# Layer 1 attention heads: TensorE's projections and scores in another order

## The chip, the cores and the metric

The kernel runs on one core of one Trainium2 chip. The metric is the device time of one execution in microseconds (us), given as the median of several runs. The five engines of the core work through their own instruction lists in order and meet at semaphores: PE is TensorE (matmuls, and PEld its weight loads), DVE is VectorE, ACT is ScalarE, POOL is GpSimd and SP issues the DMAs.

## The reference, cut to what matters

Four transformer layers follow one another, each an attention block and a feed-forward block on a normalised x. The change touches only the attention of layer 1: 16 heads of 128 features, on one sequence of 1024 tokens with 256 features, with rotary embedding and a window of 128 tokens.

```python
q = split_heads(hidden_states @ wq)
k = split_heads(hidden_states @ wk)
v = split_heads(hidden_states @ wv)
q = _apply_rotary(q, cos, sin)
k = _apply_rotary(k, cos, sin)
attn = jnp.einsum('bhqd,bhkd->bhqk', q, k) * scale
attn = jnp.where(valid, attn, neg)          # valid: the 128 keys up to the query
attn = jax.nn.softmax(attn, axis=-1)
out = jnp.einsum('bhqk,bhkd->bhqd', attn, v)
return out @ wo
```

## The kernel before, in words

The order of everything is written out by hand, one list for each engine. The 16 heads of layer 1 are a loop over pairs of heads. `c` is 0 for the even head of a pair and 1 for the odd one. While head h is finished, the queries and keys of head h+1 are made, so one pass of `head` holds steps of two heads. The last head has no next one.

On TensorE these are the steps of one pass:

- `project_qk(h + 1, j)`, j = 0 to 3: keys of tokens 0 to 511 (j = 0), queries of the same tokens (1), keys and queries of tokens 512 to 1023 (2, 3). Each is six matmuls of 512 columns on fp32r operands (a value is split in a high and a low part, three products for each half of the 256 features; lines 486 to 488). It writes bank j % 2, so only banks 0 and 1 of PSUM are used: j = 2 must find bank 0 read out, j = 3 bank 1. That is the wait on `rope_half`, which VectorE raises.
- `scores(h, gs)`, four groups g of 256 queries, in fp32, into bank 2 + g % 2 (line 649). Groups 0 and 1 of head h are made in the pass before, groups 2 and 3 in its own.
- `turn_probs(h, g)`: transposes of the exponentials (line 663), into bank 4 or 5.
- `weigh_values(h, ..., g)`: probabilities times values in fp32 (lines 678, 679), into bank 6 or 7.
- `project_out(h, p)`, four parts of six fp32r matmuls of 256 columns, and in the odd heads `project_v` of the next pair, four parts of twelve (lines 486 to 488 again).

VectorE's list for one pass is: `row_max(h, 2)`, `rotate(h + 1, 0)`, `row_max(h, 3)`, `rotate(h + 1, 1)`, in the heads 0 to 9 a step of the expert selection of layer 1 (`choose`), `rotate(h + 1, 2)`, `rotate(h + 1, 3)`, the reciprocal, `rest_of_oT` twice, `row_max(h + 1, 0)` and `(h + 1, 1)`, in the heads 0 to 9 a second `choose` step, and four `add_head`, which add the head's output to x. `row_max` (line 1406) takes a group of scores out of its bank. `rotate` (lines 1396 and 1397) reads a projection out of bank j % 2 and raises `rope_half` when it is done; it also waits for ScalarE's `keep_raw` (line 1030), a copy of the same bank. GpSimd adds the two halves of the rotation (lines 1733, 1738) and raises `qk_ready`, for which the scores wait.

ScalarE's list is: exponentials of group 0 and 1 (line 1049), `keep_raw(h + 1, 0)`, exponentials of group 2, `keep_raw(h + 1, 1)`, `keep_pT` 0 and 1, exponentials of group 3, `keep_raw` 2, `keep_pT` 2, `keep_raw` 3, `keep_oT` 0, `keep_pT` 3, `keep_oT` 1.

Of the kernel before, what the change touches and what calls it, by code (L numbers as in the profile page):

```python
# [81 lines left out]
def build(nc, dram, out):  # L82

    ctx = ExitStack()
    with ctx:
# [48 lines left out]
        def parts(pair):  # L134

            return [t.bitcast(F32R) for t in pair]
# [25 lines left out]
        def first(n):  # L162

            return isinstance(n, int) and n == 0
# [281 lines left out]
        def _(pe):  # L446
# [32 lines left out]
            def tok(t):  # L479
                return slice(t * P, (t + 1) * P)  # L480

            def split_product(dst, terms, open_end=False):


                for n, ((lhi, llo), (rhi, rlo)) in enumerate(terms):
                    pe.matmul(dst, lhi, rhi, start=(n == 0), stop=False)  # L486
                    pe.matmul(dst, lhi, rlo, start=False, stop=False)  # L487
                    last = pe.matmul(dst, llo, rhi, start=False, stop=(n == len(terms) - 1 and not open_end))  # L488
                return last

            def cut(pair, *at):
                return [t[at] for t in pair]
# [122 lines left out]
            def project_qk(h, j, pair=None):  # L615

                mm, b = 1 - j % 2, j // 2
                if j == 0:
                    pe.wait_ge(wqk_split, h + 1)
                if j < 2 and pair is not None:  # L620
                    pe.wait_ge(v1_ready, pair * 4 + (3 + j))
                elif j >= 2 or not first(h):
                    pe.wait_ge(rope_half, h * 4 + (j - 1))
                split_product(ps[j % 2], [(cut(parts(wqk2), ALL, tok(mm * KD + k)), cut(parts(xT1), ALL, k, slice(b * BW, (b + 1) * BW)))
                                          for k in range(KD)]).then_inc(qk_full, 1)

            def project_v(pair, p):

                if p == 0:
                    pe.wait_ge(wv_split, pair + 1)  # L630
                if p < 2:
                    pe.wait_ge(rope_half, pair * 8 + (3 + p))
                else:
                    pe.wait_ge(v1_ready, pair * 4 + (p - 1))
                for tt in range(2):
                    last = split_product(ps[p % 2][:, tt * D:(tt + 1) * D], [(cut(parts(xT1), ALL, k, tok(2 * p + tt)), cut(parts(wv2), ALL, k))
                                                                             for k in range(KD)])
                last.then_inc(v_full, 1)

            def scores(h, gs):  # L640

                for g in gs:
                    pe.wait_ge(qk_ready, h * 4 + (2 if g < 2 else 4))
                    if g >= 2:
                        pe.wait_ge(smax_ready, h * 4 + (g - 1))
                    for tt in range(2):
                        t = 2 * g + tt
                        lo = P if t == 0 else 0
                        last = pe.matmul(ps[2 + g % 2][:, tt * 2 * P + lo:(tt + 1) * 2 * P], qT1[:, tok(t)],  # L649
                                         kT1[:, t * P - P + lo:t * P + P], start=True, stop=True)  # L650
                    last.then_inc(bank_full[2 + g % 2], 1)

            def turn_probs(h, g):
                pe.wait_ge(exp_done, h * 4 + (g + 1))
                if g < 2:
                    pe.wait_ge(x_added, h * 4 + (HEAD0["added"] - 1 + g))
                else:
                    pe.wait_ge(pT_ready, h * 4 + (g - 1))
                for tt in range(2):
                    for s in range(2):  # L660
                        t = 2 * g + tt
                        if t or s:
                            last = pe.transpose(ps[4 + g % 2][:, tok(2 * tt + s)], S1[:, t, tok(s)], ident)  # L663
                last.then_inc(bank_full[4 + g % 2], 1)

            def weigh_values(h, pair, c, g):

                mine = slice(c * DH, (c + 1) * DH)
                pe.wait_ge(pT_ready, h * 4 + (g + 1))
                if g % 2 == 0:  # L670
                    pe.wait_ge(*HEAD0["left"][6 + g // 2])
                    pe.wait_ge(x_added, h * 4 + (HEAD0["added"] - 3 + g // 2))
                if g == 0:
                    pe.wait_ge(v1_ready, pair * 4 + 4)
                for tt in range(2):
                    t = 2 * g + tt
                    if t:
                        pe.matmul(ps[6 + g // 2][:, tok(t % TPB)], v1[:, t - 1, mine], pT1[:, t, 0, :], start=True, stop=False)  # L678
                    last = pe.matmul(ps[6 + g // 2][:, tok(t % TPB)], v1[:, t, mine], pT1[:, t, 1, :], start=(t == 0), stop=True)  # L679
                if g % 2:  # L680
                    last.then_inc(bank_full[6 + g // 2], 1)

            def project_out(h, p):

                if p == 0:
                    pe.wait_ge(wo_split, h + 1)
                if p < 2:
                    pe.wait_ge(oT1_ready, h * 2 + (p + 1))
                if p == 2:
                    pe.wait_ge(oT1_ready, h * 2 + 2)  # L690
                bank = OUT1[p]
                for tt in range(2):
                    last = split_product(ps[bank][:, tt * D:(tt + 1) * D], [(cut(parts(oT1), ALL, tok(2 * p + tt)), parts(wo2p))])
                last.then_inc(bank_full[bank], 1)

            def head(pair, c, more=True, more_v=True):

                h, next_pair = pair * 2 + c, None if c else pair
                if more:
                    project_qk(h + 1, 0, next_pair)  # L700
                scores(h, [2])
                if more:
                    project_qk(h + 1, 1, next_pair)
                turn_probs(h, 0)
                turn_probs(h, 1)
                scores(h, [3])
                if more:
                    project_qk(h + 1, 2)
                weigh_values(h, pair, c, 0)
                turn_probs(h, 2)  # L710
                if more:
                    project_qk(h + 1, 3)
                weigh_values(h, pair, c, 1)
                turn_probs(h, 3)
                weigh_values(h, pair, c, 2)
                weigh_values(h, pair, c, 3)
                if c and more_v:
                    project_v(pair + 1, 0)
                if more:
                    scores(h + 1, [0, 1])  # L720
                for p in range(NT // 2):
                    project_out(h, p)
                    if c and more_v and p < NT // 2 - 1:
                        project_v(pair + 1, p + 1)
# [26 lines left out]
            with pe.Fori(0, H1 // 2 - 1) as i:  # L751
                for c in range(2):
                    head(i, c)
            head(H1 // 2 - 1, 0)
            head(H1 // 2 - 1, 1, False, False)


# [1176 lines left out]
```

## Time and profile before

| | before |
|---|---|
| median of 3 runs | 828.32 us (827.7, 828.32, 833.49) |
| span of the profiled execution | 825.5 us |
| mean granted TensorE clock over the span | 0.968 |
| PE busy | 751.2 us, 91% of the span |
| DVE, ACT, POOL busy | 554.4, 371.9, 339.0 us |

The profiled execution is told by its span, from its first to its last instruction; the time of that same execution around the span is not given apart. The median of the runs is 2.8 us above this span. All times below are in microseconds from the start of the span. The passes of heads 0 to 14, those with a next head, run from 257.78 to 560.8. TensorE counts as busy nearly without a break there, but its matmuls are pipelined and the ends of its records are modelled, so that a record's duration can cover a wait; the starts of consecutive records tell more.

### The profile page before, as it was taken

The numbers are of one execution on the slowest core, as the hardware profiler recorded it, in microseconds if no ns is written. First come the engines' busy times: TensorE is split into PE (matmuls) and PEld (weight loads), VectorE is DVE, ScalarE is ACT, GpSimd is POOL, SyncE is SP. The second block draws the span as 40 slices with busy tenths as digits, with TensorE's granted clock in tenths as the row PEclk, the third lists the DMA queues.
The fourth block names the chain that finished last, engine by engine and source line by source line (L and its number), as shares of the span: only waits on it lengthen the run. The fifth ranks groups of instructions, "written<-read, shape, count | busy, mean of one in ns | idle before, by whom it ended". The sixth has DMA issues, their size and how long they took to land.

```text
span 825.5 us, 12512 instructions
## 1 busy us (share of the span) xinstructions
PE 751.2 (91%) x4180; PEld 590.4 (72%) x4180; DVE 554.4 (67%) x1101; ACT 371.9 (45%) x783; POOL 339.0 (41%) x250
## 2 busy tenths in 40 slices
PE   6999999999979999999999999998999799766467
PEld 2456676667838898989898999997889446455356
DVE  4454554632269979797979675755566844499995
ACT  2554111101146565656565656555455441475541
POOL 0000364420046757575757584843111110337661
PEclk9999999999999999999999999999999999977798
DMA  8300000000040100010100010101110000100001
GB/s 315 154 0 1 1 1 1 1 1 0 1 147 2 27 25 27 24 28 23 28 23 27 24 51 6 33 7 37 41 38 0 0 1 0 33 0 1 0 1 51
DMA packets 11167, 24.33 MB, mean 29 GB/s; under 512 B 1217, under 2 KB 5442, under 8 KB 10626
## 3 DMA queue, kind: packets, MB, share of 16 engines
q1 hardware_dynamic: 10832, 23.02, 8.3%
q10 hardware_dynamic: 306, 0.92, 0.5%
q8 instruction: 18, 0.29, 0.1%
q14 instruction: 11, 0.09, 0.0%
HBM read 22.89 MB, written 1.05 MB: 29 GB/s over the span
## 4 chain that ended last, share of the span: by engine, by line
PE 68%; DVE 21%; issue 7%; ACT 2%; DMA 1%; POOL 1%; DVEq 1%; SPq 0%; ACTq 0%; POOLq 0%
PE bank L467 11%; PE bank L486 8%; PE bank L488 8%; PE bank L487 8%; PE bank L476 7%; PE bank L649 4%; PE bank L556 3%; PE bank L542 3%; PE bank L679 2%; PE bank L504 2%; PE bank L678 2%; DVE x L1422 2%; PE bank L663 2%; PE bank L525 2%; DVE arena L1396 2%
## 5 line engine op out<-in xcount | busy, mean ns | idle before, releaser
L486 PE MATMUL bank<-zone 128*128 128x256 f32 (+1 forms) x520 | 180.2, 346 | 9.2 <-DVE arena L1397 3.9
L488 PE MATMUL bank<-zone 128*128 128x256 f32 (+1 forms) x520 | 169.5, 326 | 0.0
L487 PE MATMUL bank<-zone 128*128 128x256 f32 (+1 forms) x520 | 169.3, 326 | 0.0
L486 PEld LDWEIGHTS bank<-zone 128*128 128x128 f32 x520 | 99.2, 191 | 26.7 <-DVE arena L1397 9.4
L1733 POOL TENSOR_TENSOR arena<-arena 128x512 f32<-128x512 f32 x64 | 82.2, 1284 | 84.4 <-ACT arena L1030 75.5
L488 PEld LDWEIGHTS bank<-zone 128*128 128x128 f32 x520 | 99.1, 191 | 8.7
L487 PEld LDWEIGHTS bank<-zone 128*128 128x128 f32 x520 | 99.4, 191 | 6.6
L1738 POOL TENSOR_TENSOR arena<-arena 128x512 f32<-128x512 f32 x64 | 82.4, 1288 | 33.1 <-DVE arena L1397 23.0
L1727 POOL TENSOR_TENSOR zone<-arena,zone 128x512 fp32r<-128x512 f32 (+1 forms) x56 | 58.6, 1059 | 58.9 <-ACT zone L1092 46.2
L467 PE MATMUL bank<-xT,arena 128*128 128x512 f32 x160 | 77.1, 611 | 0.0
L1049 ACT ACTIVATE arena<-arena 128x256 f32<-128x256 f32 (+1 forms) x128 | 62.1, 487 | 32.9 <-DVE arena L1406 32.8
L1710 POOL TENSOR_TENSOR lnw<-lnw,minus_half 128x4 f32<-128x4 f32 x8 | 8.1, 1015 | 134.8 <-DVE lnw L1234 134.8
L1422 DVE SCALAR_TENSOR_TENSOR x<-bank,arena,x 128x256 f32<-128x256 f32 x128 | 53.0, 471 | 15.0 <-PE bank L488 14.7
L1406 DVE CUSTOM_DVE_ANT_0 arena<-bank,const 128x256 f32<-128x256 f32 (+1 forms) x128 | 46.2, 403 | 24.4 <-PE bank L649 24.2
L869 PE MATMUL bank<-zone 128*128 128x512 f32 x128 | 39.2, 463 | 25.4 <-DVE arena L1609 21.4
L649 PE MATMUL bank<-arena 128*128 128x256 f32 (+1 forms) x256 | 59.8, 366 | 0.0
L1396 DVE TENSOR_TENSOR arena<-bank,arena 64x512 f32<-64x512 f32 x64 | 44.3, 693 | 16.3 <-ACT arena L1030 14.8
L869 PEld LDWEIGHTS bank<-zone 128*128 128x128 f32 x128 | 27.9, 226 | 35.3 <-DVE arena L1609 23.8
L1719 POOL TENSOR_TENSOR arena<-arena 128x1024 bf16<-128x1024 bf16 x6 | 12.8, 2128 | 95.3 <-DVE arena L1343 95.3
L979 ACT ACTIVATE arena<-bank 128x512 f32<-128x512 f32 x16 | 9.6, 597 | 90.8 <-PE bank L467 90.8
L679 PE MATMUL bank<-arena 128*128 128x128 f32 x256 | 49.5, 275 | 0.7 <-ACT arena L1017 0.7
L1030 ACT ACTIVATE arena<-bank 128x512 f32<-128x512 f32 x64 | 37.5, 586 | 24.9 <-PE bank L488 24.9
(268 smaller groups left out, 1530.4 us busy)
## 6 DMA issues: line engine op xcount, KB each, us to landing
arena<-in_qk SPq DMA_DIRECT2D x16, 256.0 KB, 2.7
arena<-in_tern SPq DMA_DIRECT2D x1, 3072.0 KB, 20.3
arena<-in_wv SPq DMA_DIRECT2D x8, 256.0 KB, 2.6
arena<-in_wo SPq DMA_DIRECT2D x16, 128.0 KB, 2.0
arena<-in_w SPq DMA_DIRECT2D x8, 256.0 KB, 2.7
lB<-in_lB SPq DMA_DIRECT2D x1, 1288.5 KB, 22.9
arena<-in_lA SPq DMA_DIRECT2D x1, 1282.5 KB, 13.6
x<-in_x SPq DMA_DIRECT2D x1, 1024.0 KB, 11.0
```

Of the source, the lines that this page charges most:

```text
L467: last = pe.matmul(g.ps, weight(k), act[:, k, b * BW:(b + 1) * BW], start=(k == 0), stop=(k == KD - 1))
L486: pe.matmul(dst, lhi, rhi, start=(n == 0), stop=False)
L487: pe.matmul(dst, lhi, rlo, start=False, stop=False)
L488: last = pe.matmul(dst, llo, rhi, start=False, stop=(n == len(terms) - 1 and not open_end))
L649: last = pe.matmul(ps[2 + g % 2][:, tt * 2 * P + lo:(tt + 1) * 2 * P], qT1[:, tok(t)], kT1[:, t * P - P + lo:t * P + P], start=True, stop= ...
L679: last = pe.matmul(ps[6 + g // 2][:, tok(t % TPB)], v1[:, t, mine], pT1[:, t, 1, :], start=(t == 0), stop=True)
L869: last = pe.matmul(g.ps, weight, part[:, k, b * BW:(b + 1) * BW], start=(k == 0 and m == 0), stop=(k == KD - 1 and m == 1))
L1049: last = act.activation(S1[:, t, lo:], S1[:, t, lo:], ACT.Exp, scale=-1.0, bias=nmax[:, t:t + 1], accum_out=rsum[:, t:t + 1])
L1396: dve.tensor_tensor(qsin[0:64, j, :], ps[j % 2][64:128, :], sinT[64:128, at], ALU.mult)
L1422: last = dve.scalar_tensor_tensor(out=x[:, t, :], in0=ps[bank][:, tt * D:(tt + 1) * D], scalar=rinv[:, t:t + 1], in1=x[:, t, :], op0=ALU.m ...
L1733: pool.tensor_tensor(qraw[:, j, :], qraw[:, j, :], cosT[:, at], ALU.mult).then_inc(cos_done, 1)
L1738: pool.tensor_tensor((kT1, qT1)[j % 2][:, at], qraw[:, j, :], qsin[:, j, :], ALU.add).then_inc(qk_ready, 1)
```

## The change

Only TensorE's list is touched; the other engines' lists, the semaphores, the buffers and every matmul stay as they are. Three things move in a pass: `project_qk` 1 comes right behind `project_qk` 0, ahead of the score group 2; `project_qk` 3 comes right behind `project_qk` 2, ahead of `weigh_values` 0 and `turn_probs` 2; and the next head's score groups 0 and 1 come ahead of the first part of the value projection, which makes a difference in the odd heads alone.

```diff
                 if more:
                     project_qk(h + 1, 0, next_pair)
+                    project_qk(h + 1, 1, next_pair)
                 scores(h, [2])
-                if more:
-                    project_qk(h + 1, 1, next_pair)
                 turn_probs(h, 0)
                 turn_probs(h, 1)
                 scores(h, [3])
                 if more:
                     project_qk(h + 1, 2)
+                    project_qk(h + 1, 3)
                 weigh_values(h, pair, c, 0)
                 turn_probs(h, 2)
-                if more:
-                    project_qk(h + 1, 3)
                 weigh_values(h, pair, c, 1)
                 turn_probs(h, 3)
                 weigh_values(h, pair, c, 2)
                 weigh_values(h, pair, c, 3)
+                if more:
+                    scores(h + 1, [0, 1])
                 if c and more_v:
                     project_v(pair + 1, 0)
-                if more:
-                    scores(h + 1, [0, 1])
```

The first place is TensorE at the head of a pass. Here before: projection 0 ends in bank 0, the two score matmuls of group 2 go to bank 2, projection 1 goes to bank 1, and the transposes begin.

```order
L488 MATMUL bank0<-zone 128x512
L643 ISA
L645 REGISTER_ALU
L649 MATMUL bank2<-arena 128x256 x2
L621 REGISTER_ALU
L486 MATMUL bank1<-zone 128x512
L487 MATMUL bank1<-zone 128x512
L488 MATMUL bank1<-zone 128x512
L486 MATMUL bank1<-zone 128x512
L487 MATMUL bank1<-zone 128x512
L488 MATMUL bank1<-zone 128x512
L656 REGISTER_ALU
```

The score group stood between the two projections. The same place in the changed kernel:

```order
L488 MATMUL bank0<-zone 128x512
L621 REGISTER_ALU
L486 MATMUL bank1<-zone 128x512
L487 MATMUL bank1<-zone 128x512
L488 MATMUL bank1<-zone 128x512
L486 MATMUL bank1<-zone 128x512
L487 MATMUL bank1<-zone 128x512
L488 MATMUL bank1<-zone 128x512
L643 ISA
L645 REGISTER_ALU
L649 MATMUL bank2<-arena 128x256 x2
L656 REGISTER_ALU
```

Score group 2 now stands behind all twelve projection matmuls and right ahead of the transposes. The second place is TensorE in the middle of the pass. Before, the end of projection 2 (bank 0) is followed by `weigh_values` 0 (bank 6) and `turn_probs` 2 (bank 4), and then by projection 3 (bank 1).

```order
L488 MATMUL bank0<-zone 128x512
L672 REGISTER_ALU
L679 MATMUL bank6<-arena 128x128
L678 MATMUL bank6<-arena 128x128
L679 MATMUL bank6<-arena 128x128
L654 REGISTER_ALU
L663 MATMUL bank4<-const,arena 128x128 x4
L623 REGISTER_ALU
L486 MATMUL bank1<-zone 128x512
```

Four other steps' worth of small matmuls lay between the two projections. In the changed kernel:

```order
L488 MATMUL bank0<-zone 128x512
L623 REGISTER_ALU
L486 MATMUL bank1<-zone 128x512
L487 MATMUL bank1<-zone 128x512
L488 MATMUL bank1<-zone 128x512
L486 MATMUL bank1<-zone 128x512
L487 MATMUL bank1<-zone 128x512
L488 MATMUL bank1<-zone 128x512
L672 REGISTER_ALU
L679 MATMUL bank6<-arena 128x128
```

Only the wait on `rope_half` (the row of line 623) stands between them now. The third place is the end of an odd head's pass in the changed kernel, from the last matmul of `weigh_values` 3 on; before, the score groups of the next head (line 649) stood twelve matmuls later, behind the first part of the value projection (bank 0).

```order
L679 MATMUL bank7<-arena 128x128
L649 MATMUL bank2<-arena 128x128
L649 MATMUL bank2<-arena 128x256
L649 MATMUL bank3<-arena 128x256 x2
L630 REGISTER_ALU
L632 ISA
L486 MATMUL bank0<-zone 128x256
```

The scores are ahead of the projection into bank 0 there; nothing else moved.

## Rows read from the trace of the kernel before

**Rows 1.** The page's chain that ended last: shares of the span by engine.
```profile
PE 68%; DVE 21%; issue 7%; ACT 2%; DMA 1%; POOL 1%; DVEq 1%; SPq 0%; ACTq 0%; POOLq 0%
```
**Rows 2.** Stretches (window, length, busy time by engine, granted clock, DMA share, GB/s).
```profile
480.00:520.00 40.00, 40.00 (x270) 36.48 (x270) 26.50 (x72) 24.76 (x65) 25.75 (x22) 1.00 0.08 26
560.00:600.00 40.00, 36.54 (x224) 31.85 (x224) 22.52 (x55) 21.80 (x42) 8.60 (x9) 1.00 0.14 40
640.00:660.00 20.00, 14.33 (x80) 8.48 (x80) 16.27 (x48) 9.50 (x13) 2.93 (x3) 0.91 0.00 0
```
**Rows 3.** Waits of the weight loads, 257 to 560: total us, times, longest.
```profile
PEld bank L486 <- DVE arena L1397: 8.0, 15, 1.0
```
**Rows 4.** Timeline of TensorE, head 12: start, us, engine, line, operation.
```profile
504.03 0.40 PE L486 MATMUL bank<-zone 128*128 128x512 f32 x1
...
505.42 1.02 PE L649 MATMUL bank<-arena 128*128 128x256 f32 x4
506.09 0.58 PE L486 MATMUL bank<-zone 128*128 128x512 f32 x1
506.51 0.39 PE L487 MATMUL bank<-zone 128*128 128x512 f32 x1
...
507.67 0.93 PE L663 MATMUL bank<-const,arena 128*128 128x128 f32 x7
508.43 1.03 PE L649 MATMUL bank<-arena 128*128 128x256 f32 x4
509.44 0.50 PE L486 MATMUL bank<-zone 128*128 128x512 f32 x1
509.77 0.39 PE L487 MATMUL bank<-zone 128*128 128x512 f32 x1
```
**Rows 5.** Score matmuls: three in a row; and all from 300 to 580 (min/median/max ns).
```profile
254.64 0.81 PE L649 MATMUL bank<-arena 128*128 128x256 f32 x3
...
L649 PE MATMUL bank<-arena x216: 270/379/383, 300.8 to 563.6; 128*128 128x256 f32 x95, 128*128 128x128 f32 x13
```
**Rows 6.** Timeline of VectorE, head 12, and ScalarE's second copy there (idle time in brackets).
```profile
506.63 0.42 DVE L1406 CUSTOM_DVE_ANT_0 arena<-bank,const 128x256 f32<-128x256 f32 x1 [1.43 <-PE bank L649]
...
507.99 0.69 DVE L1396 TENSOR_TENSOR arena<-bank,arena 64x512 f32<-64x512 f32 x1 [0.58 <-ACT arena L1030]
508.70 0.68 DVE L1397 TENSOR_TENSOR arena<-bank,arena 64x512 f32<-64x512 f32 x1
509.65 0.42 DVE L1406 CUSTOM_DVE_ANT_0 arena<-bank,const 128x256 f32<-128x256 f32 x1 [0.27 <-PE bank L649]
...
510.46 0.69 DVE L1396 TENSOR_TENSOR arena<-bank,arena 64x512 f32<-64x512 f32 x1
...
508.76 0.58 ACT L1030 ACTIVATE arena<-bank 128x512 f32<-128x512 f32 x1
```
**Rows 7.** Timeline of TensorE, ends of the passes of head 8 and head 12.
```profile
435.66 1.68 PE L649 MATMUL bank<-arena 128*128 128x128 f32 x8
437.27 0.39 PE L486 MATMUL bank<-zone 128*128 128x256 f32 x1
...
440.12 0.28 PE L488 MATMUL bank<-zone 128*128 128x256 f32 x1
440.41 0.49 PE L486 MATMUL bank<-zone 128*128 128x512 f32 x1
...
516.65 1.68 PE L649 MATMUL bank<-arena 128*128 128x128 f32 x8
517.98 0.47 PE L486 MATMUL bank<-zone 128*128 128x256 f32 x1
```
**Rows 8.** Timelines of VectorE and TensorE, head 9.
```profile
444.67 0.40 DVE L1406 CUSTOM_DVE_ANT_0 arena<-bank,const 128x256 f32<-128x256 f32 x1
...
446.16 0.68 DVE L1397 TENSOR_TENSOR arena<-bank,arena 64x512 f32<-64x512 f32 x1
...
446.90 0.50 PE L486 MATMUL bank<-zone 128*128 128x512 f32 x1 [0.58 <-DVE arena L1397]
```

## The prediction

> **What bounds the kernel now.** I read the page's chain first: TensorE holds 68% of it [rows 1]. Then the stretches: in the heads of layer 1 TensorE is busy for all of a 40 us window at a granted clock of 1.00 (2.4 GHz), while VectorE fills 26.5 us and ScalarE and GpSimd less [rows 2]. So what TensorE waits there is added to the total, and what it saves is taken off. Then the waits: the one that recurs is line 486, the first matmul of a projection, on line 1397, the end of VectorE's `rotate`; 15 times, 8.0 us in weight loads, much of it hidden by the matmul in flight [rows 3]. It is the wait for a free bank 0 or 1, and this is the wait whose surroundings the change rearranges. So I lay out TensorE's and VectorE's starts in one pass, head 12.
>
> **Units, from head 12.** A projection takes 505.42 - 504.03 = 1.39 us for six matmuls, 0.232 each [rows 4]. A score record takes (0.81 - 0.38) / 2 = 0.215, so a group of four 0.85 [rows 5]. The seven transposes of `turn_probs` 0 and 1 take 508.43 - 507.67 = 0.76 [rows 4]. On VectorE, from `row_max` to the `rotate` behind it is 510.46 - 509.65 = 0.81, and a `rotate` takes 508.70 + 0.68 - 507.99 = 1.39. `row_max` 3 starts 0.37 after the score group's last record is through (508.43 + 0.85 = 509.28, to 509.65) [rows 4, 6]. The projection that waited for `rotate` 0 (end 509.38) has its second matmul at 509.77, so it ran as if begun at 509.54: 0.16 after the release [rows 4, 6].
>
> **Part 1, fewer changes between fp32 and fp32r: nothing.** The change takes away two turns in each direction in an even pass and three in an odd one. Where fp32r follows fp32, the first matmul is 0.42 ahead of the second (506.09 to 506.51) where 0.232 is usual, which looks like a cost of 0.19. But from the start of the score group to the second matmul is 1.09 (505.42 to 506.51), and 0.85 + 0.23 = 1.08 accounts for that [rows 4, 5]: the record merely begins early. So I take 0 a turn; the bounds are 0 and 0.19, and fewer turns can't cost. With two turns back to fp32r saved in each of 8 even passes and three in each of 7 odd ones, 37 in all, the upper bound is 7.0 us gained.
>
> **Part 2, `project_qk` 1 ahead of score group 2.** The matmuls are the same, so the transposes still begin at 507.67. But score group 2 ends there instead of at 505.42 + 0.85 = 506.27, 1.40 later. VectorE has `row_max` 2 at the head of its list, and `rotate` 0 queued behind it, though projection 0 has long been ready. `row_max` 2 begins at 507.67 + 0.37 = 508.04, `rotate` 0 at 508.85 (ScalarE's copy for it is done before 507.99 [rows 6], so it no longer waits for that) and ends at 510.24. Projection 2, which needs bank 0, can run from 510.40. Transposes and score group 3 leave TensorE free at 509.28. The wait is 1.12 where 0.26 (509.54 - 509.28) stands now: **+0.86**.
>
> **Part 3, `project_qk` 3 right behind `project_qk` 2.** VectorE goes from `rotate` 0 into `row_max` 3 (0.81) and `rotate` 1 (1.39), some 2.2 us a round against a projection of 1.39. `rotate` 1 ends at 510.24 + 2.22 = 512.46, projection 3 can run from 512.62; projection 2 is over at 511.79: **+0.83**. Before, `weigh_values` 0 and `turn_probs` 2 filled this gap. ScalarE's second copy is no later link: it ended at 509.34, 1.9 after `row_max` 2 (507.44) [rows 6], and 508.85 + 1.9 = 510.75 is ahead of `rotate` 1 at 511.07. Behind projection 3 the smaller work comes in the same length as before, and ScalarE's copies for it have more time, except `keep_raw` 3, which now waits in ScalarE's list behind `keep_pT` 2; the latter can only begin after `turn_probs` 2. That makes `rotate` 3 later by about what TensorE is later; I cost it 0, with the last score groups of the pass (1.33 long before the next record starts [rows 7]) as cover for `rest_of_oT`.
>
> **Part 4, score groups ahead of `project_v` 0 (odd heads).** Same matmuls in another order at a full engine; their input, the rotated first two projections, was begun before all the small work of the pass, and their exponentials are needed only by the transposes of the next pass. 0; bounds -0.2 to +0.2 in 7 passes, 1.4 us either way.
>
> **The sum over the 15 passes.** For the five passes without `choose` (heads 10 to 14) I take 0.86 + 0.83 = 1.69 each: 8.5 us. In the five even passes with `choose` (0 to 8) the same 1.69 arises, but two waits at the end are there because VectorE and GpSimd come late relative to TensorE, and a later TensorE swallows them: the output projection starts 1.61 after the scores began in head 8 against 1.33 in head 12 (0.28), and the next head's first projection 0.29 after the last matmul instead of 0.12 (0.17) [rows 7]. Left: 1.24 each, 6.2 us. In the five odd passes with `choose` (1 to 9) VectorE reaches `row_max` 2 only at 444.67, having been busy until then with the adds. With the changed order score group 2 would be read from 440.41 + 2 x 1.39 + 0.85 + 0.37 = 444.41, so nothing is late there, and projection 2 waits for `rotate` 0 (end 446.84, start 446.90) as now [rows 8]. Only part 3 counts: 0.83 each, 4.2 us. Total 8.5 + 6.2 + 4.2 = **+18.9 us**. The profiled span would be 825.5 + 18.9 = 844.4, and with the 2.8 us between it and the median of 828.3, the forecast is **847.2 us**. Bounds of the size: if VectorE's lateness in the `choose` passes swallows half their terms, 13.7 us (842.0); if the odd `choose` passes pay all 1.69, and every pass 0.3 for `keep_raw` 3, 27.7 us (856.0).
>
> **The skill against the trace.** Banks 0 and 1 alternate in both kernels; in the changed one two waits of about 1 us stand where VectorE is emptying them. The Trainium skill, "Perfetto Trace Analysis", section Matmuls, asks that independent matmul groups rotate through banks so that the emptying of one overlaps the next group's matmuls. By that rule closer pairs alone would be harmless if bank 1 were free when bank 0 is done; the 2.2 us round on VectorE against 1.39 on TensorE [rows 4, 6] says two banks aren't enough here, and the sum goes by the rows.
>
> **Rivals.** (a) The turns between types do cost 0.19, and the waits come as well: 18.9 - 7.0 = +11.9, 840.2 us. For it speaks the 0.42 us record spacing; against it, that the sum of starts closes without it. (b) The other side: `rotate` isn't late. If TensorE's longer block of projections let VectorE finish `rotate` 0 within the 0.76 + 0.85 = 1.61 us of transposes and score group 3, the waits would be gone and only the saved turns would count: 828.3 - 7.0 = 821.3 us. It decides at 1.61 us from the end of score group 2 to the release of bank 0; the rows give 0.37 + 0.81 + 1.39 + 0.16 = 2.73, so it would need VectorE to take `rotate` 0 first, which its list doesn't do. (c) The clock. In 640 to 660 TensorE is busy for 14.33 of 20 us and the granted clock averages 0.91; if the new pauses did that to the heads, some 300 us of matmuls would take 300 / 0.91 - 300 = 30 us more on top of the forecast, 877 us. Against it: from 560 to 600 it is busy 36.54 of 40 and the clock stays at 1.00 [rows 2]; the 303 us of passes before the change (head 0 to 14) would become some 322 with at most 303 of work, 94% or a little less, no emptier than that. The Trainium skill, "TensorE: Matmul & The Clock Gate", section A second HAM failure mode, tells of a clock that swings because of short pauses between matmul groups; that is this rival. (d) The order has no effect, the waits being hidden in depth that I don't see: 828 us. TensorE's order does change, and its records sit back to back, so I see no room.
>
> **How the numbers follow.** Forecast 0.81 (838 to 857), (a) 0.08, (b) 0.02, (c) 0.05, (d) 0.04. The range 838 to 857 takes in the bounds of the sum and (a), and leaves out (b), (c), (d) and a remainder. A change of 1% (8.3 us) is about what a measurement of this kernel can tell from none: faster 0.02, within 1% 0.06, slower 0.92.
>
> **What would show it.** In the changed profile the waits of line 486 on line 1397 grow to about two a pass, 1.1 and 0.8 us; in an even pass without `choose` the next head's scores begin 14.3 us after the first projection instead of 516.65 - 504.03 = 12.6; `row_max` 2 starts 1.4 later relative to the pass's start. Wrong would be: the first matmul of projection 3 following projection 2 without a gap, a clock under 1.00 between 258 and 580, or passes shorter than before. Most fragile is the share that the `choose` passes swallow.

## The result and the profile after

The changed kernel takes 847.21 us (median of 6 runs, 845.95 to 850.74) against 828.53 us for the kernel before (6 runs): ratio 1.0226, 95% interval 1.0200 to 1.0251. It is slower by 18.7 us; the forecast was 847.2 us. The profiled execution took 847.81 us with a span of 845.9 us.

The waits of TensorE in the heads' stretch, from 257 to 582 us (who waited, for whom, total us, times, longest), now have one line that dwarfs the rest. VectorE's `rotate` has become lines 1394 and 1395, `row_max` line 1404, since the file is two lines shorter.

```profile
PE bank L486 <- DVE arena L1395: 19.6, 30, 0.8
PEld bank L486 <- DVE arena L1395: 32.1, 30, 1.2
```

Thirty waits are two in each of the 15 passes; before, the weight loads had 15 of them with 8.0 us in total [rows 3]. TensorE's timeline of head 12 (start, us, engine, line, operation, idle time in brackets), which answers to [rows 4]:

```profile
517.31 0.40 PE L486 MATMUL bank<-zone 128*128 128x512 f32 x1
...
520.05 1.03 PE L649 MATMUL bank<-arena 128*128 128x256 f32 x4
520.91 0.93 PE L663 MATMUL bank<-const,arena 128*128 128x128 f32 x7
521.68 1.03 PE L649 MATMUL bank<-arena 128*128 128x256 f32 x4
523.52 0.50 PE L486 MATMUL bank<-zone 128*128 128x512 f32 x1 [0.81 <-DVE arena L1395]
523.86 0.40 PE L487 MATMUL bank<-zone 128*128 128x512 f32 x1
...
525.75 0.50 PE L486 MATMUL bank<-zone 128*128 128x512 f32 x1 [0.58 <-DVE arena L1395]
526.09 0.40 PE L487 MATMUL bank<-zone 128*128 128x512 f32 x1
```

VectorE in the same head, which answers to [rows 6], and ScalarE's first copy (`keep_raw` 0) there:

```profile
520.57 0.57 ACT L1028 ACTIVATE arena<-bank 128x512 f32<-128x512 f32 x1
...
521.27 0.42 DVE L1404 CUSTOM_DVE_ANT_0 arena<-bank,const 128x256 f32<-128x256 f32 x1 [2.79 <-PE bank L649]
...
522.08 0.69 DVE L1394 TENSOR_TENSOR arena<-bank,arena 64x512 f32<-64x512 f32 x1
522.78 0.68 DVE L1395 TENSOR_TENSOR arena<-bank,arena 64x512 f32<-64x512 f32 x1
523.50 0.42 DVE L1404 CUSTOM_DVE_ANT_0 arena<-bank,const 128x256 f32<-128x256 f32 x1
...
524.31 0.69 DVE L1394 TENSOR_TENSOR arena<-bank,arena 64x512 f32<-64x512 f32 x1
525.01 0.68 DVE L1395 TENSOR_TENSOR arena<-bank,arena 64x512 f32<-64x512 f32 x1
```

VectorE sits idle for 2.79 us until score group 2 is through, and then works without a gap through `row_max` 2, `rotate` 0, `row_max` 3 and `rotate` 1. Projection 0 has been in its bank since 518.70 (517.31 + 1.39), but `rotate` 0 also needs ScalarE's copy of it, which ended at 521.14. So `rotate` 0, begun at 522.08, was ready only some 0.9 us earlier: what it loses is the length of the `row_max` ahead of it, not the whole idle time. Projection 2 starts 0.06 after the first `rotate` ends (522.78 + 0.68 = 523.46), projection 3 0.06 after the second (525.69). The recorded idle of TensorE (0.81 and 0.58) is less than the real wait, because a record lasts longer than its share of the array. By starts: score group 3 is over at 521.68 + 0.85 = 522.53 and projection 2 ran as if begun at 523.86 - 0.23 = 523.63, a wait of 1.10; it was over at 525.02 and projection 3 ran from 525.86, a wait of 0.84. The forecast had 1.12 and 0.83.

The lengths of the passes, from the first record of projection 0 to the next head's, worked out from TensorE's timelines of all runs of this study (medians of the passes of a kind, in us; for these kernels they agree within 0.04 from head to head, head 0 aside, except in the passes with `choose` of the fifth row, where they spread over more than 1 us; the last column is the sum of passes 0 to 13):

```
                           choose           no choose       heads 0-13
                         even    odd       even    odd
before                   17.38   23.85     17.01   22.76    286.0
changed                  18.74   24.50     18.76   24.50    302.8
first pair alone         17.95   23.84     17.82   23.57    292.1
second pair alone        18.16   24.50     18.17   23.92    297.6
rotate first             21.2    27.0      21.2    24.0     325.3
scores first alone       17.38   23.83     17.02   22.76    286.0
more turns               17.38   23.86     17.03   22.75    286.1
both lists               18.44   23.82     18.44   22.90    294.1
both lists, old order    18.37   23.56     18.37   22.83    292.2
rotates ahead            18.37   23.74     18.37   22.56    291.5
scalar list tuned        16.86   23.99     16.85   22.48    283.3
same, old order          16.87   23.33     16.80   22.50    279.9
```

Head 14 is an even pass without `choose` and adds one more; the last head, which projects nothing, began at 560.78 before and at 579.31 after, 18.5 us later. So the heads alone account for 18.5 of the 20.4 us between the two spans. The other 1.9 us lie behind them, in the experts that follow. There this execution's clock fell, as TensorE's timeline shows:

```profile
594.57 0.40 PE L488 MATMUL bank<-zone 128*128 128x512 f32 x1
594.80 0.45 PE L486 MATMUL bank<-zone 128*128 128x512 f32 x1
...
595.47 0.63 PE L488 MATMUL bank<-zone 128*128 128x512 f32 x1
595.90 0.63 PE L486 MATMUL bank<-zone 128*128 128x512 f32 x1
```

The stretch behind it (window, its length, busy time of PE, PEld, DVE, ACT and POOL, granted clock, DMA share, GB/s):

```profile
596.00:599.00 3.00, 3.00 (x10) 2.37 (x9) 0.00 (x0) 0.36 (x1) 0.00 (x0) 0.60 0.16 39
```

The same matmul starts every 0.43 us instead of 0.23, which is the 1.2 GHz level instead of 2.4, for eight matmuls, 8 x 0.2 = 1.6 us. TensorE had waited three times in the 7 us before (0.70, 1.20 and 0.66 of recorded idle). In the profiled execution of the kernel before, the same place, with the same three waits (0.70, 1.20, 0.65), ran at a granted clock of 1.00. Nor does the fall need the change: of the kernels below, the one with the scores first alone, whose passes are as long as before, has it there too.

```profile
576.00:579.00 3.00, 3.00 (x10) 2.39 (x9) 0.00 (x0) 0.00 (x0) 0.00 (x0) 0.61 0.48 161
```

The profiles of both lists and of the same lists tuned with TensorE's old order don't. The six times of the changed kernel spread over 4.8 us, the longest at a mean granted clock of 0.961, the shortest at 0.969.

### The profile page after: what moved, and what is told of

Read it like the earlier page. It is cut to its first block, busy times and chain, and to the rows that moved or that the text cites. A ratio compares the mean times of both kernels' runs of the same rounds, so it can differ in the third digit from the quotient of the medians.

```text
span 845.9 us, 12512 instructions
## 1 busy us (share of the span) xinstructions
PE 755.8 (89%) x4180; PEld 591.2 (70%) x4180; DVE 555.2 (66%) x1101; ACT 369.4 (44%) x783; POOL 337.5 (40%) x250
## 4 chain that ended last, share of the span: by engine, by line
PE 67%; DVE 22%; issue 6%; ACT 2%; POOL 1%; DVEq 1%; DMA 1%; SPq 0%; ACTq 0%; POOLq 0%
PE bank L467 11%; PE bank L486 8%; PE bank L487 7%; PE bank L488 7%; PE bank L476 7%; PE bank L679 3%; PE bank L678 3%; PE bank L556 3%; PE bank L542 3%; DVE arena L1404 3%; PE bank L504 3%; DVE arena L1394 3%; PE bank L649 3%; DVE x L1420 2%; DVE arena L1395 2%
## 5 line engine op out<-in xcount | busy, mean ns | idle before, releaser
L1394 DVE TENSOR_TENSOR arena<-bank,arena 64x512 f32<-64x512 f32 x64 | 44.3, 692 | 20.6 <-ACT arena L1028 18.9
L977 ACT ACTIVATE arena<-bank 128x512 f32<-128x512 f32 x16 | 9.6, 597 | 90.8 <-PE bank L467 90.8
L649 PEld LDWEIGHTS bank<-arena 128*128 128x128 f32 x256 | 43.6, 191 | 4.4
```

The lines of the kernel that those rows point to most:

```text
L1394: dve.tensor_tensor(qsin[0:64, j, :], ps[j % 2][64:128, :], sinT[64:128, at], ALU.mult)
```

## The experiments

All medians are beside runs of the kernel before on the same chip (829.0 to 829.3 us). None of these kernels leaves out part of the computation.

**First pair alone.** The kernel before with projection 1 moved ahead of score group 2.

```diff
                 if more:
                     project_qk(h + 1, 0, next_pair)
+                    project_qk(h + 1, 1, next_pair)
                 scores(h, [2])
-                if more:
-                    project_qk(h + 1, 1, next_pair)
```

> The kernel before with one part of the change: the first two projections together, score group 2 behind them. Theory (VectorE's list makes the release of banks 0 and 1 late): projection 2 of a pass waits about 1.1 us instead of 0.26, projection 3 not at all, because the end of projection 2 plus the 1.1 us of small matmuls (509.54 + 0.86 + 1.39 + 1.11 = 512.90) is later than 512.62. Plus 0.86 in the five passes without choose, about 0.4 in the even passes with choose (two waits at their end shrink), 0 to 0.3 in the odd ones: 6.3 to 8 us, 835 to 836.5 us. Rival (turns between types cost 0.19 each): one turn to fp32r less in 15 passes, 2.9 us less than that, 832 to 833.5. Rival (no effect): 828.5.

Measured: 838.06 us, ratio 1.0121 (1.0081 to 1.0161). The passes show the theory's terms: +0.81 us without `choose` (0.86 expected), +0.57 in the even passes with it (about 0.4), 0.00 in the odd ones, 6.9 us in all with head 14. TensorE in head 12:

```profile
512.48 1.03 PE L649 MATMUL bank<-arena 128*128 128x256 f32 x4
514.32 0.50 PE L486 MATMUL bank<-zone 128*128 128x512 f32 x1 [0.81 <-DVE arena L1396]
514.66 0.40 PE L487 MATMUL bank<-zone 128*128 128x512 f32 x1
...
516.48 0.60 PE L663 MATMUL bank<-const,arena 128*128 128x128 f32 x4
516.84 0.48 PE L486 MATMUL bank<-zone 128*128 128x512 f32 x1
```

Projection 2 waits 1.10 (514.43 less 513.33), and projection 3, behind four transposes of 0.11 each, doesn't wait at all. The median of four runs, which spread over 6.1 us, is 1.6 us above the expected times; the profiled execution, from which the passes are read, took 836.05 us and lies within them. So the remainder isn't shown to come from the heads; where it arose stays open.

**Second pair alone.** Projection 3 moved right behind projection 2, score group 2 in its old place.

```diff
                 if more:
                     project_qk(h + 1, 2)
+                    project_qk(h + 1, 3)
                 weigh_values(h, pair, c, 0)
                 turn_probs(h, 2)
-                if more:
-                    project_qk(h + 1, 3)
```

> The kernel before with one part of the change: projection 3 right behind projection 2, score group 2 in its old place. Theory: rotate 1 ends at 511.85 as before, projection 2 at 510.93, so projection 3 waits 1.08 us; the wait of projection 2 stays at 0.26. Plus 1.1 in the five passes without choose, 1.1 less the 0.45 of waits at the end in the even passes with choose, 0.83 in the odd ones: 5.4 + 3.2 + 4.2 = 12.8 us, 841.3 us. Rival (turns): 2.9 us less, 838.4. If the waits of the two parts only add up together, this run alone shows much less than 12.

Measured: 841.34 us, ratio 1.0146 (1.0124 to 1.0169). TensorE in head 12:

```profile
519.28 0.40 PE L488 MATMUL bank<-zone 128*128 128x512 f32 x1
520.48 0.51 PE L486 MATMUL bank<-zone 128*128 128x512 f32 x1 [0.81 <-DVE arena L1396]
520.82 0.39 PE L487 MATMUL bank<-zone 128*128 128x512 f32 x1
```

Projection 2 is over at 519.51 and projection 3 ran as if begun at 520.59: a wait of 1.08, as worked out. Without `choose` a pass is 1.16 longer, with it 0.78 (even, where 0.65 was expected) and 0.65 (odd, where 0.83 was expected). So each pair costs by itself. Without `choose` the two apart (0.81 + 1.16 = 1.97) come to a little more than the 1.75 of the changed kernel: there projection 2 itself begins later, and projection 3 waits 0.84 instead of 1.08.

**Scores first alone.** The third move by itself.

```diff
+                if more:
+                    scores(h + 1, [0, 1])
                 if c and more_v:
                     project_v(pair + 1, 0)
-                if more:
-                    scores(h + 1, [0, 1])
```

> The kernel before with one part of the change: in the odd passes the next head's score groups 0 and 1 ahead of the first part of the value projection. Theory: same matmuls in another order on a full TensorE, 0, 828.5 us, bounds 1.4 either way. Rival (turns): one turn to fp32r less in 7 passes, 1.3 us less, 827.2. The odd pass in the trace, 22.76 us long in head 11 before, tells the two apart better than the time: 22.76 or 22.57.

Measured: 828.92 us, ratio 0.9999 (0.9977 to 1.0021), and 22.75 and 22.77 us for the odd passes without `choose`, 22.76 before. It does nothing that these runs can show.

**More turns.** The rival that a turn between fp32 and fp32r costs 0.19 us was the only source of a gain, so it was measured by itself.

```diff
+                for n in range(4):
+                    product(n)
...
+                pe.matmul(ps[6][:, tok(0)], v1[:, 0, mine], pT1[:, 0, 1, :], start=True, stop=True)
+                product(4)
+                pe.matmul(ps[6][:, tok(1)], v1[:, 0, mine], pT1[:, 1, 0, :], start=True, stop=False)
+                product(5)
+                pe.matmul(ps[6][:, tok(1)], v1[:, 1, mine], pT1[:, 1, 1, :], start=False, stop=True)
```

> The kernel before with the cost of the turns between fp32 and fp32r measured by itself: the last two of projection 2's six matmuls are put between the three matmuls of weigh_values 0 (same matmuls, same banks, the same total). Two turns to fp32r and two back are added in each of the 15 passes, none of the large waits moves. Theory (a turn costs nothing): the same time, 828.5 us, and an even pass without choose stays at 17.0 us. Rival (0.19 a turn): 30 turns to fp32r, 5.7 us more, 834.2 us, and that pass 17.4 us.

Measured: 828.89 us, ratio 0.9998 (0.9975 to 1.0021). TensorE in head 12 (line 703 is fp32r, 714 to 718 fp32):

```profile
515.97 0.39 PE L714 MATMUL bank<-arena 128*128 128x128 f32 x2
516.11 0.48 PE L703 MATMUL bank<-zone 128*128 128x512 f32 x1
516.43 0.39 PE L716 MATMUL bank<-arena 128*128 128x128 f32 x2
516.57 0.48 PE L703 MATMUL bank<-zone 128*128 128x512 f32 x1
516.89 0.38 PE L718 MATMUL bank<-arena 128*128 128x128 f32 x2
```

From one fp32 matmul to the next are 0.46 us: 0.23 for the projection's matmul and 0.22 for the fp32 one, the usual lengths. Four turns a pass were added and the passes kept their lengths to 0.02 us, so a turn costs at most some 5 ns here. The record of 0.48 us that looked like a price is a start written early.

**Rotate first.** The changed kernel with VectorE's list turned round, to see whether `row_max` ahead of `rotate` is the whole cause. In this and all runs below TensorE also waits, ahead of score groups 0 and 1, for the `row_max` of the group before in their bank (`if g >= 2 or not first(h)`), which the old list implied.

```diff
                 for g in (2, 3):
-                    row_max(h, g)
                     if more:
                         rotate(h + 1, g - 2)
+                    row_max(h, g)
```

> The changed kernel with VectorE's list turned round in one place: rotate 0, row_max 2, rotate 1, row_max 3. (One wait is added on TensorE, which is always satisfied: score groups 0 and 1 wait for the row_max of the group before in their bank, as the old order implied.) Theory, worked out from the trace's durations: projection 2 is released as in the kernel before (wait 0.26 in an even pass, 0 in an odd one), but ScalarE's second copy stands behind the exponentials of group 2, which need row_max 2, which now stands behind rotate 0; so rotate 1 can start only at about 511.85 in head 12's terms and projection 3 waits 2.5 us in an even pass and 1.4 in an odd one. Even passes about 19.4 us, odd ones about 24.0; total about 848 us, no better than the changed kernel. If instead the row_max alone made the lateness, the waits of projection 2 and 3 both go and the time falls to 828 or below.

Measured: 869.67 us, ratio 1.0510 (1.0475 to 1.0545), far worse than the 848 expected. TensorE's timeline in head 12, and the start of VectorE's `rotate` 1:

```profile
542.37 1.03 PE L649 MATMUL bank<-arena 128*128 128x256 f32 x4
543.40 0.50 PE L486 MATMUL bank<-zone 128*128 128x512 f32 x1
543.74 0.40 PE L487 MATMUL bank<-zone 128*128 128x512 f32 x1
...
545.89 0.69 DVE L1394 TENSOR_TENSOR arena<-bank,arena 64x512 f32<-64x512 f32 x1 [1.73 <-ACT arena L1028]
...
547.33 0.71 PE L486 MATMUL bank<-zone 128*128 128x512 f32 x1 [2.27 <-DVE arena L1395]
547.84 0.63 PE L487 MATMUL bank<-zone 128*128 128x512 f32 x1
548.27 0.63 PE L488 MATMUL bank<-zone 128*128 128x512 f32 x1
```

The wait of projection 2 is back from 1.10 to 0.29 us (543.51 less 543.22), near the 0.26 of the kernel before: it was `row_max` 2 ahead of `rotate` 0. The wait moved to projection 3, since `rotate` 1 now waits for ScalarE's second copy. Projection 2 is over at 544.89 and projection 3 ran as if begun at about 547.41, 2.5 us later, as worked out. What wasn't expected is that TensorE's clock fell behind this wait.

The stretches around it, in the columns of the stretch above:

```profile
544.00:547.00 3.00, 1.06 (x5) 0.54 (x3) 1.25 (x4) 2.50 (x8) 2.03 (x2) 1.00 0.00 0
547.00:550.00 3.00, 2.67 (x7) 2.09 (x8) 1.05 (x5) 1.88 (x7) 1.79 (x3) 0.57 0.00 0
```

After a stretch with TensorE busy for 1.06 of 3 us the matmuls start 0.43 apart. This is the clock rival of the forecast, which the heads of the changed kernel, with waits of 1.1 and 0.8 us, stayed clear of. The even passes without `choose`, 4.2 us longer than before, are 2.5 us of wait and eight steps of TensorE that take 0.2 us more each, 1.6 us for the clock.

**Both lists.** The changed kernel with VectorE at `rotate` 0, `row_max` 2, `rotate` 1, `row_max` 3, and ScalarE turned to it.

```diff
                 for g in range(4):
+                    if more and g == 0:
+                        keep_raw(h + 1, 0)
+                    if g == 2:
+                        if more:
+                            keep_raw(h + 1, 1)
+                        keep_pT(h, 0)
+                        keep_pT(h, 1)
...
-                    if more and g == 1:
-                        keep_raw(h + 1, 0)
-                    if g == 2:
-                        if more:
-                            keep_raw(h + 1, 1)
-                        keep_pT(h, 0)
-                        keep_pT(h, 1)
```

> The changed kernel's TensorE order with the lists of both readers turned to it: VectorE rotate 0, row_max 2, rotate 1, row_max 3; ScalarE copy 0 ahead of all exponentials of the pass, copy 1 and keep_pT 0 and 1 ahead of the exponentials of groups 2 and 3 (and the same added wait on TensorE). Theory: rotate 0 ends about 1.6 us after projection 0, rotate 1 before projection 2 is over, no wait of projections 2 and 3 is left. Even pass without choose 16.7 us (17.01 before, 18.76 changed), odd 22.4 (22.76, 24.50); the passes with choose gain the lateness of VectorE as well, even 16.8 to 17.2, odd 22.4 to 23. Heads 0 to 14 together 8 to 11 us shorter than in the kernel before: 818 to 821 us. Rival (the pair of projections in a row is in itself too close for two banks): waits of 0.8 us stay at projection 3, 830 or more.

Measured: 836.40 us, ratio 1.0094 (1.0072 to 1.0117). 818 to 821 us were expected, so the time missed. The two waits on `rotate` are gone without `choose` (in head 12 projection 2 is over at 518.81 and projection 3 begins at 518.81), so two banks aren't in themselves too few; five waits of up to 0.6 us of recorded idle are left, in the passes with `choose`. But a new wait arose in the even passes. ScalarE and TensorE in head 12:

```profile
512.20 1.28 ACT L1028 ACT_TABLE_LOAD   x1 [1.57 <-PE bank L488]
513.49 0.60 ACT L1028 ACTIVATE arena<-bank 128x512 f32<-128x512 f32 x1
513.98 0.39 ACT L1054 ACTIVATE arena<-arena 128x128 f32<-128x128 f32 x1
...
515.09 0.54 PE L663 MATMUL bank<-const,arena 128*128 128x128 f32 x3 [0.77 <-ACT arena L1054]
516.07 0.65 PE L663 MATMUL bank<-const,arena 128*128 128x128 f32 x4 [0.44 <-ACT arena L1054]
```

After the value copies ScalarE loads a table, 1.28 us. In the kernel before, the load began 0.09 us after the pass did (504.12 and 504.03) and the exponentials were done before the transposes needed them; with copy 0 first, it begins 1.65 after it (512.20 and 510.55), because it waits for projection 0, and the exponentials and the transposes wait for load and copy. By starts this holds up the transposes for 1.66 us: score group 3 begins at 516.56 instead of 513.29 + 0.85 + 0.76 = 514.90.

**Both lists, old order.** The same lists with TensorE in the order of the kernel before (the other two moves are taken back in the same way).

```diff
                 if more:
                     project_qk(h + 1, 0, next_pair)
-                    project_qk(h + 1, 1, next_pair)
                 scores(h, [2])
+                if more:
+                    project_qk(h + 1, 1, next_pair)
...
```

> The same lists of VectorE and ScalarE and the same added wait, but TensorE in the order of the kernel before. It tells whether anything of a gain belongs to TensorE's new order. Theory: the waits of projections 2 and 3 go here too, and since turns between types cost nothing the time is that of the run with TensorE's new order, within 2 us, 818 to 821. Rival: the new order is worth something once it isn't waited for, and this one is slower by the turns, 37 of 0.19 us, 7 us.

Measured: 832.59 us, ratio 1.0053 (1.0036 to 1.0071). The same table load holds it (0.74 and 0.44 of idle in head 12), so it missed as well; but it is no slower than its twin with the new order, against the rival.

**Rotates ahead.** VectorE `rotate` 0 and 1, then `row_max` 2 and 3; ScalarE both copies behind exponentials 1.

```diff
-                for g in (2, 3):
-                    row_max(h, g)
-                    if more:
-                        rotate(h + 1, g - 2)
+                if more:
+                    rotate(h + 1, 0)
+                    rotate(h + 1, 1)
+                row_max(h, 2)
+                row_max(h, 3)
```

> The changed kernel's TensorE order with VectorE rotate 0, rotate 1, row_max 2, row_max 3, and ScalarE exponentials 0 and 1, copies 0 and 1, keep_pT 0 and 1, exponentials 2 and 3. Theory: in an even pass copy 0 stands behind two exponentials and the table load, so rotate 0 ends at 509.38 in head 12's terms and the wait of 0.26 stays; rotate 1 ends at 510.8, ahead of need. Even pass without choose 17.0 us, odd 22.4; total 4 to 8 us under the kernel before, 820 to 824, slower than the run with copy 0 first by about 3 us.

Measured: 833.06 us, ratio 1.0059 (1.0031 to 1.0086). The odd passes without `choose` fell to 22.56, near the 22.4 forecast; the even ones are 18.37 instead of 17.0. Head 12, ScalarE's tail and TensorE:

```profile
519.66 0.57 ACT L1028 ACTIVATE arena<-bank 128x512 f32<-128x512 f32 x1
520.14 0.58 ACT L1017 ACTIVATE arena<-bank 128x512 f32<-128x512 f32 x1
...
520.84 0.48 PE L678 MATMUL bank<-arena 128*128 128x128 f32 x2 [0.70 <-ACT arena L1017]
```

The late `row_max` makes the exponentials of groups 2 and 3 late, and `keep_pT` 2 (line 1017), queued behind them and the rounding of the weights, is what `weigh_values` 2 waits for, 0.96 us by starts. `weigh_values` 3 then waits again, 0.22 us of recorded idle, for `keep_pT` 3.

**Scalar list tuned.** From these misses: the first exponentials ahead of copy 0, so that the table load is out of the way, and copy 3 and `keep_pT` 2 in the order of need. VectorE as in both lists.

```diff
+                exponentials(h, 0)
+                raw(0)
+                exponentials(h, 1)
+                raw(1)
+                keep_pT(h, 0)
+                keep_pT(h, 1)
+                exponentials(h, 2)
+                raw(2)
+                exponentials(h, 3)
+                raw(3)
                 round_wo(h)
-                if more_v and not c:
-                    round_wv(pair + 1)
...
                 keep_pT(h, 2)
                 keep_oT(h, 0)
                 keep_pT(h, 3)
+                if more_v and not c:
+                    round_wv(pair + 1)
                 keep_oT(h, 1)
```

> The changed kernel's TensorE order, VectorE rotate 0, row_max 2, rotate 1, row_max 3, and a new list of ScalarE: exponentials 0, copy 0, exponentials 1, copy 1, keep_pT 0 and 1, exponentials 2, copy 2, exponentials 3, copy 3, round_wo, keep_pT 2, keep_oT 0, keep_pT 3, round_wv, keep_oT 1. The first exponentials of an even pass load their table (1.28 us) behind the value copies again, ahead of copy 0, so that it costs nothing on the way to the transposes; in the earlier runs with turned lists the table load or copy 2 ahead of keep_pT 2 made TensorE wait. Theory (the readers' lists make every wait there is): no wait of projections 2 and 3 left, 0.15 at weigh_values 3; even pass without choose 16.8 us, odd 22.4; passes with choose about 17.0 and 23.0, because VectorE still comes late from the adds in the odd ones. 6 to 8 us less than the kernel before, 821 to 823. Rival (something else holds a pass of 17.0): no gain, 828.

Measured: 824.99 us, ratio 0.9965 (0.9946 to 0.9983), 2 us above the 821 to 823 expected. Even passes are 16.86, odd ones without `choose` 22.48, as expected; the odd ones with it are 23.99 where 23.0 was expected. Head 9, TensorE:

```profile
445.71 0.40 PE L488 MATMUL bank<-zone 128*128 128x512 f32 x1
446.68 0.50 PE L486 MATMUL bank<-zone 128*128 128x512 f32 x1 [0.57 <-DVE arena L1400]
```

There VectorE comes from the adds only at 443.00 and the pair of projections pays for its round again, 0.84 us.

**The same with TensorE's old order.** All three moves are taken back (the cut shows the second), and one copy of ScalarE goes behind `keep_pT` 2 to fit it.

```diff
                 if more:
                     project_qk(h + 1, 2)
-                    project_qk(h + 1, 3)
                 weigh_values(h, pair, c, 0)
                 turn_probs(h, 2)
+                if more:
+                    project_qk(h + 1, 3)
...
                 exponentials(h, 3)
-                raw(3)
                 round_wo(h)
                 keep_pT(h, 2)
+                raw(3)
```

> The same with TensorE in the order of the kernel before, and in ScalarE's list round_wo and keep_pT 2 ahead of copy 3, since there the transposes come ahead of projection 3. Theory: the same waits gone, and turns between types cost nothing, so within 2 us of the run with TensorE's new order. If TensorE's new order is worth something in itself once the lists fit it, this one is slower by that.

Measured: 822.05 us, ratio 0.9927 (0.9898 to 0.9955), the fastest kernel here and 7 us under the kernel before. All kinds of passes agree with the run above within 0.05 us but the odd ones with `choose`, 23.33 against 23.99. Head 9 again:

```profile
444.57 0.60 PE L663 MATMUL bank<-const,arena 128*128 128x128 f32 x4
444.93 0.48 PE L486 MATMUL bank<-zone 128*128 128x512 f32 x1
```

The transposes cover VectorE's round and projection 3 doesn't wait. So even with lists fitted to each, TensorE's new order has no merit here: it costs 5 x 0.66 = 3.3 us, and the medians differ by 2.9 (less than 2 was expected).

## Why the prediction was right, point by point

**Part 1, turns between types cost nothing:** shown by the runs with more turns and with the scores first: the ratios are 0.9998 and 0.9999, with intervals of 0.2% either way, and the passes are unchanged to 0.02 us, where rival (a) asked for 0.4 and 0.19. Rival (a) falls.

**Part 2, +0.86:** shown alone by the first run, where projection 2 waits 1.10 us and the passes without `choose` are 0.81 longer. Turning only `row_max` 2 and `rotate` 0 round brought that wait back to 0.29, which shows its cause. Of the 0.05 between 0.86 and 0.81, 0.02 is the wait itself (1.10, not 1.12); the rest isn't traced. The prediction's words that projection 0 "has long been ready" hold for the bank alone: in the changed kernel ScalarE's copy ended 0.13 us before `row_max` 2 began.

**Part 3, +0.83:** the wait in the changed kernel is 0.84. That VectorE's round of 2.2 us is longer than a projection of 1.39 is shown from both sides: the wait exists with score group 2 in its old place (1.08), and it goes in the passes without `choose` when the copies and `rotate` 1 are ready earlier.

**Part 4, nothing:** shown by the run with the scores first.

**The sum.** Forecast +18.9, measured +18.5 in the heads and +18.7 between the medians. Its terms, head by head: without `choose` 1.69 forecast, 1.75 measured. Even passes with `choose` 1.24 forecast, 1.37 measured (1.12 in head 0). Odd ones 0.83 forecast, 0.65 measured. The step with the largest error is the last: it held that VectorE reaches `row_max` 2 as late as before, so that only part 3 would count. In the changed kernel the even pass ahead of it is 1.4 us longer and VectorE is less late. Head 9, VectorE, beside its start at 449.55:

```profile
450.40 3.20 DVE L1420 SCALAR_TENSOR_TENSOR x<-bank,arena,x 128x256 f32<-128x256 f32 x8
453.53 0.41 DVE L1404 CUSTOM_DVE_ANT_0 arena<-bank,const 128x256 f32<-128x256 f32 x1
```

`row_max` 2 begins 3.98 after the pass's start instead of 4.26 (444.67 less 440.41, [rows 7, 8]). The old wait of projection 2 shrinks by these 0.28, while projection 3 waits 0.84 as forecast; the 0.09 between 0.56 and 0.65 isn't traced. So the swallowing happened partly in the odd passes instead of the even ones, and the two errors nearly cancelled. That the forecast agreed with the median to 0.1 us is luck beyond that: the six times of the changed kernel alone lie between 845.95 and 850.74 us, and a fall of the clock at one place behind the heads is worth 1.6 us.

**The rivals.** (b), VectorE in time, needed 1.61 us from score group 2 to the release; it was 522.53 + 1.10 - (520.05 + 0.85) = 2.73, as the rows before gave. (c), the clock, did not come in the heads, where the granted clock over 257.7 to 576 was 1.00, but it is real: it came in the heads when one wait grew to 2.5 us. (d) falls with the result.

## What to carry to other kernels

When one engine is full and two banks pass between it and a reader, the small work that stands between two users of the banks isn't clutter but cover; before joining like with like, compare the reader's whole round, everything queued in it, with the length of one producer step. A wait on an in-order reader is set by what stands ahead in its list, so a producer's order and its readers' lists have to be moved together, and each list turned alone may only exchange one wait for another. Judge such changes by the lengths of the repeated passes in the trace, which here agree within 0.04 us while the clock stays up, rather than by whole times that scatter by 2.5 to 6.5 us.

## What the runs showed of the hardware

A change between fp32 and fp32r matmuls in a full stream costs nothing measurable (0.02 us in a pass with four more of them); a matmul's recorded start can lie up to 0.2 us ahead of its share of the array (0.42 and 0.48 us records in a stream of 0.23 and 0.22). TensorE's clock stayed at 2.4 GHz with two waits of 1.1 and 0.8 us in every 19 us, and fell to 1.2 GHz for some three microseconds behind a wait of 2.5 us. Behind the heads, after waits of 0.70, 1.20 and 0.66 us of recorded idle, it fell in some profiled executions and not in others. The Trainium skill, "TensorE: Matmul & The Clock Gate", section HAM oscillation, warns of long idle gaps of TensorE; here 2.27 us of recorded idle, in a stretch with TensorE busy for 1.06 of 3 us, were followed by a granted clock of 0.57. And ScalarE's table load of 1.28 us comes at the first exponential or copy behind the value copies of each even pass. With copy 0 first it was part of a delay of 1.66 us; with an exponential first, in the scalar list tuned, the even pass of 16.86 us shows no such delay.
